# A transformer layer in bf16 on eight cores: residual output through staging tiles, stores issued one tile later, bf16 intermediates

## What is computed

```python
x = x + layernorm(attn(layernorm(x)))
x = x + layernorm(ffn(layernorm(x)))
```

```python
scores = einsum('bnshd,bnshd->bnsh', Qs, Ks) * 64 ** -0.5   # q . k of the same position
probs = softmax(scores, axis=2)                              # over the 128 positions
attn = probs[..., None] * Vs                                 # other offsets stay zero
out = attn @ Wo + bo
```

```python
h = silu(x @ wg.T) * (x @ wu.T)
out = h @ wd.T
```

## Time and profile before

| | us |
|---|---|
| median of the runs | 4249.15 (4223.15 and 4275.15) |
| profiled execution, its time | 3977.53 |
| its span on the slowest core, core 4 | 3976.0 |
| spans of the eight cores | 3930.7 to 3976.0 |
| PE busy | 2714.8 (68%) |
| DVE busy | 1037.1 (26%) |
| ACT busy | 832.1 (21%) |
| POOL busy | 275.6 (7%) |

### The profile page before, as it was taken

How to read it: one execution, slowest core, us unless ns; L and a number is a source line. 1 busy time by engine, 2 the same in 40 slices (tenths; PEclk the granted TensorE clock), 3 DMA queues, 4 the chain that set the end, 5 groups by cost and what they waited for, 6 DMA issues and landing times.

```text
span 3976.0 us, 36052 instructions; the slowest of 8 cores (3930.7 to 3976.0 us)
## 1 busy us (share of the span) xinstructions
PE 2714.8 (68%) x12651; PEld 1284.3 (32%) x12867; DVE 1037.1 (26%) x1908; ACT 832.1 (21%) x1569; POOL 275.6 (7%) x245
## 2 busy tenths in 40 slices
PE   0223589934995569945996469934996569944995
PEld 0122234422442234422442224422442234422442
DVE  1111421134112331134212331134212331134112
ACT  0000321124111331123211331124111331124111
POOL 1110000010001000010002000010002000010001
PEclk9999578966998679966998679966998679966998
DMA  7887112441236202441125202441225202440223
GB/s 151 172 158 170 48 47 70 133 143 32 69 85 181 89 27 75 126 160 38 64 80 194 86 27 83 128 149 37 69 82 191 83 28 81 134 151 32 69 87 119
DMA packets 197135, 392.49 MB, mean 99 GB/s; under 512 B 42808, under 2 KB 55120, under 8 KB 192352
## 3 DMA queue, kind: packets, MB, share of 16 engines
q1 hardware_dynamic: 156608, 295.76, 23.9%
q0 software_dynamic: 31136, 60.88, 7.8%
q10 hardware_dynamic: 9216, 33.56, 2.1%
HBM read 356.57 MB, written 60.82 MB: 105 GB/s over the span
## 4 chain that ended last, share of the span: by engine, by line
PE 53%; DMA 14%; DVE 13%; ACT 8%; issue 6%; POOL 4%; DVEq 0%; ACTq 0%; SPq 0%; POOLq 0%
PE pg L689 17%; PE pu L695 17%; PE pd L755 9%; DMA out<-x_tm 5%; POOL x_tm L811 4%; PE pkv L400 2%; ACT xh_tm L214 2%; PE pq L400 2%; DMA x_tm<-x 2%; PE ptr L223 2%; DMA xhB<-wg 2%; DVE x_tm L446 2%; ACT t_sb L651 2%; DMA xhB<-wu 1%; DVE y_sb L768 1%
## 5 line engine op out<-in xcount | busy, mean ns | idle before, releaser
L689 PE MATMUL pg<-xhB,ring_g 128*128 128x512 bf16 x3008 | 769.9, 399 | 11.1 <-DVE xhB L230 7.5
L695 PE MATMUL pu<-xhB,ring_u 128*128 128x512 bf16 x3008 | 736.2, 385 | 3.8 <-issue 0.2
L755 PE MATMUL pd<-ring_d,h_sb 128*128 128x512 bf16 x3016 | 679.0, 382 | 56.4 <-DVE y_sb L768 24.0
L711 DVE TENSOR_TENSOR h_sb<-silu_sb,pu 128x512 bf16<-128x512 f32 x384 | 264.1, 688 | 1127.2 <-ACT silu_sb L706 1127.2
L223 PE MATMUL ptr<-identb,xh_tm 128*128 128x128 bf16 x1024 | 107.0, 271 | 546.9 <-ACT xh_tm L214 543.1
L706 ACT ACTIVATE silu_sb<-pg 128x512 f32<-128x512 f32 x384 | 229.4, 597 | 1163.4 <-PE pu L695 1115.8
L689 PEld LDWEIGHTS pg<-xhB,ring_g 128*128 128x128 bf16 x3072 | 312.0, 102 | 403.4 <-issue 100.5
L755 PEld LDWEIGHTS pd<-ring_d,h_sb 128*128 128x128 bf16 x3072 | 297.4, 98 | 437.9 <-issue 96.8
L695 PEld LDWEIGHTS pu<-xhB,ring_u 128*128 128x128 bf16 x3072 | 305.3, 99 | 378.8 <-issue 59.2
L811 POOL TENSOR_TENSOR x_tm<-t_sb,x_tm 128x1024 f32<-128x1024 f32 x64 | 150.6, 2352 | 2428.0 <-DVE bn_sb L781 2399.3
L223 PEld LDWEIGHTS ptr<-identb,xh_tm 128*128 128x128 bf16 x1024 | 83.3, 121 | 577.6 <-issue 577.4
(11 more groups left out here) (78 smaller groups left out, 1357.2 us busy)
## 6 DMA issues: line engine op xcount, KB each, us to landing
ring_d<-scr_d SPq DMA_DIRECT2D x384, 256.0 KB, 2.8
ring_g<-scr_g SPq DMA_DIRECT2D x192, 256.0 KB, 2.8
ring_u<-scr_u SPq DMA_DIRECT2D x192, 256.0 KB, 3.1
x_tm<-x POOLq DMA_DIRECT2D x64, 512.0 KB, 4.9
qkvo<-scr_q SPq DMA_DIRECT2D x32, 1024.0 KB, 5.7
qkvo<-scr_q SPq DMA_DIRECT2D x64, 512.0 KB, 7.3
out<-x_tm ACTq DMA_DIRECT2D x64, 512.0 KB, 3.4
scr_q<-qkvo SPq DMA_DIRECT2D x4, 2048.0 KB, 7.7
```

The costliest lines, as they stand in the source:

```text
L689: P.op("tensor", lambda t, slot=slot, gsl=gsl, nt=nt, kcc=kcc, pg=pg: t.matmul(pg[:, 512 * gsl:512 * gsl + 512], ring_g[:, D * slot + 128 ...
L695: P.op("tensor", lambda t, slot=slot, gsl=gsl, nt=nt, kcc=kcc, pu=pu: t.matmul(pu[:, 512 * gsl:512 * gsl + 512], ring_u[:, D * slot + 128 ...
L711: P.op("vector", lambda v, gsl=gsl, ssl=ssl, hc=hc, nt=nt, pu=pu: v.tensor_mul(h_sb[:, D * hc + 512 * nt:D * hc + 512 * nt + 512], silu_sb ...
L755: P.op("tensor", lambda t, ji=ji, j=j, hf=hf, kcc=kcc, slot=slot, pd=pd: t.matmul(pd[ji][:, 512 * hf:512 * hf + 512], h_sb[:, D * kcc + 12 ...
```

## The change

The change does four things.

- A staging tile `ostg` of three slots of 128 by 1024 f32 takes the result of the residual add; slot `j % 3` for tile j. The add waits until the slot's last store has landed (`ost_war`). The store reads the slot, and there are three store counters `dos`. The load of the next unit's tile waits for POOL's own add (`gc`), no longer for the store.
- A store is put on a list and emitted one tile later, behind the apply of the next tile. The last one of the unit is emitted behind the loop over the groups, the last one of grp 0 behind the apply of the first tile of grp 1.
- The transposes of the next unit wait for the first of the four copies of `pd` in grp 1 (`yevacG1`), no longer for the fourth.
- `q_sb`, `k_sb`, `v_sb` and `silu_sb` are bf16, no longer f32.

```diff
-        q_sb = E(nc.sbuf_tensor("q_sb", [128, 512], F32))
-        k_sb = E(nc.sbuf_tensor("k_sb", [128, 512], F32))
-        v_sb = E(nc.sbuf_tensor("v_sb", [128, 2 * 512], F32))
+        q_sb = E(nc.sbuf_tensor("q_sb", [128, 512], BF16))
+        k_sb = E(nc.sbuf_tensor("k_sb", [128, 512], BF16))
+        v_sb = E(nc.sbuf_tensor("v_sb", [128, 2 * 512], BF16))
...
-        silu_sb = E(nc.sbuf_tensor("silu_sb", [128, 2 * 512], F32))
+        silu_sb = E(nc.sbuf_tensor("silu_sb", [128, 2 * 512], BF16))
+        ostg = E(nc.sbuf_tensor("ostg", [128, 3 * D], F32))
...
-        dos = [mk(f"do{i}") for i in range(2)]
+        dos = [mk(f"do{i}") for i in range(3)]
...
-                b2war = M.get(("b2yevac", u - 1), 0)
+                b2war = M.get(("yevacG1", u - 1), 0)
...
+                pend_store = []
+
+                def emit_store(j, js4, jsl, u=u):
+                    rr, nrel = j // 2, j % 2
+                    n = nbase + nrel
+                    P.wait("scalar", gc, M[("resid4", j)])
+                    P.op("scalar", lambda s, b=b_local, n=n, rr=rr, js4=js4: s.dma_start(
+                        out=out_d[b, n * 512 + rr:(n + 1) * 512:4, :],
+                        in_=ostg[:, D * js4:D * js4 + D]), dos[js4], 16)
+                    M[("ostore", u * 8 + j)] = dos[js4].n
+                    ost_war[js4] = (dos[js4], dos[js4].n)
...
+                        if grp == 1 and ji == 0:
+                            M[("yevacG1", u)] = vc.n
...
-                        P.op("gpsimd", lambda g, j=j, jsl=jsl: g.tensor_tensor(
-                            x_tm[:, D * j:D * j + D], t_sb[:, D * jsl:D * jsl + D],
+                        js4 = j % 3
+                        if js4 in ost_war:
+                            P.wait("gpsimd", ost_war[js4][0], ost_war[js4][1])
+                        P.op("gpsimd", lambda g, j=j, jsl=jsl, js4=js4: g.tensor_tensor(
+                            ostg[:, D * js4:D * js4 + D], t_sb[:, D * jsl:D * jsl + D],
                             x_tm[:, D * j:D * j + D], ALU.add), gc)
                         M[("resid4", j)] = gc.n
-                        rr, nrel = j // 2, j % 2
-                        n = nbase + nrel
-                        P.wait("scalar", gc, M[("resid4", j)])
-                        P.op("scalar", lambda s, b=b_local, n=n, rr=rr, j=j: s.dma_start(
-                            out=out_d[b, n * 512 + rr:(n + 1) * 512:4, :],
-                            in_=x_tm[:, D * j:D * j + D]), dos[jsl], 16)
-                        M[("ostore", u * 8 + j)] = dos[jsl].n
+                        pend_store.append((j, js4, jsl))
+                        if len(pend_store) > 1:
+                            emit_store(*pend_store.pop(0))
                         if u + 1 < n_units:
-                            emit_xload(u + 1, j, (dos[jsl], M[("ostore", u * 8 + j)]))
+                            emit_xload(u + 1, j, (gc, M[("resid4", j)]))
...
+                while pend_store:
+                    emit_store(*pend_store.pop(0))
```

More of the change, by code:

```diff
@@ L827, in build_nc @@
                         M[("rst1a", u + 1)] = emit_batch_rstd(MV, 0, 4)
[L829 to L832 removed]
+                while pend_store:
+                    emit_store(*pend_store.pop(0))
+        for dsem in dos:
+            P.wait("gpsimd", dsem, dsem.n)
+            P.wait("sync", dsem, dsem.n)
         with nc.Block() as block:
```

7 lines of the change are left out of this document (2 added, 5 removed).

## The result

The changed kernel takes 3879.17 us in the median of 11 runs (3865.65 to 4166.36), the kernel before 4035.16 us in the median of 10 (3943.27 to 4275.15), and the ratio of the two is **0.981, 95% interval 0.980 to 0.983**: 1.9% faster, some 73 us of 3945. Forecast was 4140 us and a gain of 109 us, with "faster by over 2%" as the likeliest; what came is a gain of 73 us, by its middle value inside "within 2%", with an interval that reaches to 2%.

What follows compares the result with a forecast made beforehand. Bound: TensorE's hole of 44.6 us between units, about 350 us in all. 57.6 + 65 + 7.6 - 7 = 123 us off 3977.5 gives 3854; for the timed runs, 109 us off 4249 gives 4140 us, range 4050 to 4215.

Steps and rivals of the forecast that it cites:

- copies no longer late: Between units: x tile 3 loads earlier, so VectorE starts the `pd` copies when the matmuls end; 57.6 us saved.
- chain: LayerNorm of tiles 4 to 7 between units: last store's issue ends 9.3 us sooner, seven times, 65 us saved.
- tail: End of last unit, no x loads: ScalarE's 2.7 us sets the pace; last store at 19.4 us, 7.6 us saved.
- transfers closer together: grp 1 of the down projection: bunched x loads and stores delay `ring_d`, costing 1 us per unit, 7 us.
- bf16, guard: Narrower `q_sb`, `k_sb`, `v_sb`, `silu_sb` and the weaker PSUM guard on next unit's transposes: no gain taken.
- about 2.7 us ... below POOL's 3.05, so POOL sets the pace: LayerNorm chain: ScalarE needs about 2.7 us per tile, POOL 3.05 us, so adds come 3.05 us apart.
- The bounds (-15 to +36 us): Bunched transfers in grp 1: from 15 us gained if stalls vanish to 36 us lost at 331 GB/s for 4.2 MB.
- The step from 3854 to the median: From changed profiled execution to timed runs: gain 94 us at lower clock, 123 otherwise; middle 109 us gives 4140 us.
- the timed runs see the lower level less often: Rival: the changed kernel's timed runs meet the lower TensorE clock less, like the profiled execution; 3854 to 4050 us, 10%.
- The load of tile 3: Rival before grp 1's copies: this load still holds VectorE, or ring stalls eat the gain; 66 us gained, 4183 us, 10%.
- The lower clock: Rival: denser work holds TensorE's lower clock for more matmuls, making the kernel slower than before; 4331 us, 6%.
- The change gives nothing: Rival: something unseen, such as attention waiting for x tiles 4 to 7, takes the time back; 4249 us, 8%.

Runs made afterwards that it cites:

- e1_small: The kernel before with only the four bf16 buffers and the weaker PSUM guard; ratio to before 1.000 (0.998 to 1.003).
- e8_nodefer: The changed kernel with each store issued at once instead of one tile later, staging kept; ratio to before 0.988 (0.979 to 0.997).
- e4_deep: The changed kernel with twelve slots instead of four for the down weights; ratio to before 0.968 (0.963 to 0.972).
- e13_spread2: The changed kernel with grp 0's four x loads issued behind steps 8, 11, 14 and 17 of grp 1; ratio to before 0.974 (0.971 to 0.978).
- e7_defer: The kernel before with store and load of a tile issued one tile later, no staging; ratio to before 0.978 (0.969 to 0.988).
- e12_defer_deep: The kernel before with store and load issued one tile later and twelve down-weight slots, no staging; ratio to before 0.976 (0.971 to 0.981).
- e3_spread: The changed kernel with grp 0's four x loads issued behind steps 1, 5, 9 and 13 of grp 1; ratio to before 0.979 (0.973 to 0.984).
- e6_nostore: The changed kernel without the stores of tiles 0 to 3; no ratio given, grp 1 47.3 us a unit.

## Why the prediction was right or wrong, point by point

**Which steps failed.** The chain of tiles 4 to 7 was given too little time and the price of the transfers was put too low; and the base was 4249 us, where the kernel before takes 3943 to 3951 us in half of its runs. What it had right: the copies start at once, the closed gap is worth 57.6 us on core 4, and the types and the guard are worth nothing.

**Core 4's own sum.** Forecast was -123 us against its profiled execution; that core came out 117 us shorter, and the agreement is chance. 31 us of it is unit 0, in which the kernel before had a stretch at 0.81 and reached its first copies 31 us later; the change has no part in that. By terms, the rest is -86:

| term | forecast | core 4 | what was found |
|---|---|---|---|
| copies no longer late | -57.6 | -57.6 | right, to the tenth |
| chain | -65 | -47.1 | mis-sized |
| tail | -7.6 | -4.0 | mis-sized, same cause |
| transfers closer together | +7 | +22.4 | mis-sized; 30 on the mean of the cores |
| bf16, guard | 0 | 0 | right (e1_small) |
| attention and the rest | 0 | +0.3 | right |

**The chain: "about 2.7 us ... below POOL's 3.05, so POOL sets the pace".** This step failed. The 2.18 us from Ln to the end of the apply was read from the earlier trace rows, where ScalarE waits for the add and L798 therefore never runs beside it. The deferral makes the two overlap for the first time, and with two SBUF tensors as input the small operation is held until the add ends: 2.18 became about 3.5 (1.42 to 1.76 instead of 0.16 for L813), and the adds stand 3.91 to 3.96 us apart. The second half of the step was too small too: I had "some 0.1" between POOL's add and its load issue, and POOL waits 0.56. By the right numbers, in unit 0: first add at 9.2, three periods of 3.96, 2.33 for the last add and 0.46 to the normalise make 23.8, as measured. With L813 mended it is 22.3, still above 21.1, and that is the 0.56, three times. The tail failed by the same step: with L813 mended its adds come 2.7 us apart, as forecast, and it is 7.4 us shorter than before where 7.6 were forecast.

**The transfers: "I take 1 us more per unit".** Mis-sized: 7 us in all were forecast, 22 came on core 4 and 30 in the mean of the cores, 4.25 a unit. The bounds (-15 to +36 us) held; I went for the lower part because the stalls beside the `qkvo` loads at the end of grp 1 would go, and weighed the new bunch at its start too lightly. What does the harm is that 512 KB loads and stores run beside each other (every 3.9 us each here, every 5.3 in e8_nodefer) and let a ring of four 256 KB slots run dry; behind the first long wait the matmuls are slower as well. The windows of the changed kernel, core 0, columns as in the earlier trace rows:

```profile
750.30:756.00 5.70, 4.96 (x16) 1.78 (x16) 1.36 (x4) 0.00 (x0) 1.79 (x2) 0.76 0.96 278
756.00:780.60 24.60, 22.93 (x104) 9.94 (x104) 4.54 (x10) 0.50 (x2) 0.00 (x0) 1.00 0.64 194
```

In the 5.7 us the DMA engines are 0.96 busy and the granted clock is 0.76; the 16 matmuls take 4.96 us where the earlier trace rows has 3.61. Shown by e4_deep, in which depth takes the waits away, and by e13_spread2, in which loads behind the stores and further apart bring them back to those of the kernel before.

**The step from 3854 to the median.** This put the number above the range, 4140 for 3879. The 272 us between the profiled execution and the runs shown were taken as the kernel's usual time. Of its ten runs five lie at 3943 to 3951 and five at 4120 to 4275, so both kinds are usual and the two shown were of the second. The case "the timed runs see the lower level less often" (3854 to 4050) was the one that came, with 10%: seven of the eleven runs of the changed kernel lie at 3866 to 3880. That the clock makes the difference fits the later rounds, in which the slowest core of the runs of the kernel before that take 4200 us or more has a granted clock of 0.75 to 0.79, against about 0.85 in those of 3943 to 3957. The gain of 94 us that was worked out for the lower clock, and the middle of 109, are neither shown nor refuted by the runs compared here. With the right base and the terms as I had them it would have been 3945 - 123 = 3822; with the measured terms, -80 on the mean of the cores, it is 3865.

**Rivals.** The load of tile 3 no longer holds VectorE (gap 0.10 us). The lower clock didn't hold longer in the profiled execution: the granted clock is 0.856 to 0.863 on the eight cores, where it was 0.841 to 0.852, and from 1000 to 1100 us, in the gate and up matmuls of the second unit, all eight have 1.00. "The change gives nothing" is out. The slot of `ostg` was never waited for where it costs: the adds wait for the apply or for the 0.56.

**What the sum hid.** I costed staging and deferral as one chain. Asked for each alone I would have said that the load needs the staging; e7_defer shows that with the ring of 4 it doesn't, and e12_defer_deep that with a ring of 12 it does in part, with 2.7 us of gap left. And the upper bound of the transfers counted 4.2 MB, though the prediction itself has the fourth store go out only behind the copies.

## What to carry to other kernels

When an edit lets two engines overlap that took turns before, durations read from the old trace hold for the old order only: look at which operations will now run beside which, above all a VectorE operation with two SBUF inputs beside a GpSimd one. When transfers are freed of a wait they bunch; give the stream that TensorE eats more slots, or keep the loads apart from the stores, in the same edit, and add up what all streams ask for in the same 10 us. And two runs don't tell what is usual: when the profiled execution and the runs lie far apart, forecast from each and say which is which.

## What the runs showed of the hardware

- A VectorE operation on 128x1 with two SBUF tensors that starts while a GpSimd add of 128x1024 from SBUF runs takes 1490 ns in the mean, up to 2.04 us, against 160; the form with one tensor and a per-partition scalar takes 214 ns beside an add as well, and statistics of 128x512 stay at 694 ns.
- GpSimd waits 0.56 us between its own add and a DMA issue that depends on it; in e3_spread three issues that wait for nothing of that add follow it at once (1186.70 behind 1184.40 + 2.35).
- Median landing of the 512 KB loads on core 0: 5.1 us in the kernel before, 8.0 with a load and a store every 3.9 us, 6.8 with one of each every 5.3 us (e8_nodefer), 5.6 with the loads behind the stores (e13_spread2), 5.3 with no stores in grp 0 (e6_nostore).
- A multiply of 128x512 with one input in PSUM takes 688 ns with the other input in float32 or bfloat16.
